# Head softmax attention: scores in two 64-row tiles, all eight half sums added up by TensorE, heads weighed eleven by VectorE and five by GpSimd

## What is computed

```python
q = (x @ Wq.T + bq).reshape(B, S, H, D)
k = (x @ Wk.T + bk).reshape(B, S, H, D)
v = (x @ Wv.T + bv).reshape(B, S, H, D)
scores = jnp.einsum('bqnd,bknd->bnqk', q, k) / jnp.sqrt(jnp.float32(D))
attn = jax.nn.softmax(scores, axis=1)
out = jnp.einsum('bnqk,bknd->bqnd', attn, v)
...
return out @ Wo.T + bo
```

## Time and profile before

| | before |
|---|---|
| median of 3 runs | 2179.37 us (2179.27 to 2180.45) |
| the profiled execution's own time | 2181.45 us |
| its span in the trace | 2178.7 us |
| TensorE busy over the span | 1938.2 us (89%) |
| VectorE | 1730.6 us (79%) |
| GpSimd | 1475.3 us (68%) |
| ScalarE | 1245.5 us (57%) |
| mean granted TensorE clock | 0.949 |

### The profile page before, as it was taken

The page is one execution under the profiler, slowest core; times in us unless marked ns, Lnnn a source line. Parts: engine busy times, 40 slices in busy tenths (PEclk is TensorE's granted clock), DMA queues, the critical chain, the costliest instruction groups (busy, mean ns, idle before and its releaser), DMA issues. The chain is left out here.

```text
span 2178.7 us, 56000 instructions
## 1 busy us (share of the span) xinstructions
PE 1938.2 (89%) x21984; PEld 1282.7 (59%) x21984; DVE 1730.6 (79%) x2433; ACT 1245.5 (57%) x2204; POOL 1475.3 (68%) x1044
## 2 busy tenths in 40 slices
PE   1799937999957999999999999999999996399997
PEld 1566632444424777777777777777777776144443
DVE  5577675666675999999999999999999996666665
ACT  2455424666634666666666666666666664266664
POOL 3100003566564999999999999999999993065564
PEclk9999958999977999999999999999999997699998
DMA  3222205995101000000000000000000000299631
GB/s 121 83 72 71 80 5 113 181 173 131 30 0 40 13 13 13 13 14 11 16 9 16 9 16 9 17 11 15 9 6 9 6 6 1 52 175 185 140 77 39
DMA packets 95317, 108.91 MB, mean 50 GB/s; under 512 B 31600, under 2 KB 56560, under 8 KB 94704
## 3 DMA queue, kind: packets, MB, share of 16 engines
q1 hardware_dynamic: 92256, 103.91, 21.2%
q10 hardware_dynamic: 2832, 1.79, 0.3%
HBM read 88.10 MB, written 17.57 MB: 49 GB/s over the span
## 5 line engine op out<-in xcount | busy, mean ns | idle before, releaser
L1177 POOL TENSOR_TENSOR ffn_exp_sw<-ffn_exp_sg,ffn_exp_wide 128x512 f32<-128x512 f32 x256 | 324.5, 1268 | 573.0 <-DMA ffn_exp_wide<-pair_weights 370.5
L963 DVE TENSOR_REDUCE head_shift<-head_score 128x64 bf16<-128x1024 f32 x512 | 625.2, 1221 | 91.3 <-PE head_score L775 79.1
L925 ACT ACTIVATE head_ex<-head_score 128x1024 f32<-128x1024 f32 x512 | 524.7, 1025 | 188.7 <-PE head_score L797 186.9
L732 POOL TENSOR_TENSOR head_half<-head_ex 128x1024 f32<-128x1024 f32 x256 | 604.2, 2360 | 27.2 <-ACT head_ex L925 27.2
L970 DVE TENSOR_TENSOR head_ex<-head_ex,head_recp 128x1536 f32<-128x1536 f32 x256 | 446.7, 1745 | 4.8 <-ACT head_recp L897 4.8
L807 PE MATMUL head_den<-head_half,c_ident 128*128 128x128 f32 x3072 | 385.3, 275 | 2.9 <-POOL head_half L733 2.7
L807 PEld LDWEIGHTS head_den<-head_half,c_ident 128*128 128x128 f32 x3072 | 363.3, 192 | 6.5 <-POOL head_half L733 3.3
L739 POOL TENSOR_TENSOR head_ex<-head_ex,head_recip 128x512 f32<-128x512 f32 x256 | 328.9, 1285 | 15.3 <-ACT head_recip L899 7.5
L1288 DVE TENSOR_TENSOR ffn_exp_h_parts<-ffn_exp_hidden,ffn_exp_h_parts 128x512 f16<-128x512 f32 x272 | 188.1, 692 | 173.8 <-ACT ffn_exp_h_parts L1248 172.8
L797 PE MATMUL head_score<-head_shift,c_identb 128*128 128x512 bf16 x1024 | 309.9, 384 | 17.6 <-DVE head_shift L963 11.3
L775 PE MATMUL head_score<-att_b_HB,att_b_GR 96*128 96x256 f16 x2048 | 311.0, 274 | 10.4 <-DMA att_b_HB<-b_queries 9.9
(11 more groups left out here) (230 smaller groups left out, 2478.5 us busy)
## 6 DMA issues: line engine op xcount, KB each, us to landing
ffn_exp_wide<-pair_weights SPq DMA_DIRECT2D x256, 256.0 KB, 8.7
a_keys<-band_parts_k SPq DMA_DIRECT2D x14, 295.5 KB, 2.5
att_a_HB<-a_keys SPq DMA_DIRECT2D x56, 73.9 KB
a_queries<-band_parts_q SPq DMA_DIRECT2D x14, 271.5 KB, 3.1
att_a_GR<-a_queries SPq DMA_DIRECT2D x14, 271.5 KB
b_queries<-head_parts_q SPq DMA_DIRECT2D x32, 96.0 KB, 1.6
att_b_HB<-b_queries SPq DMA_DIRECT2D x128, 24.0 KB
b_keys<-head_parts_k SPq DMA_DIRECT2D x24, 96.0 KB, 1.6
```

What stands on the lines that cost most here:

```text
L732: ch.link(pool.tensor_tensor(hf, e[:, 0:8, :], e[:, 8:16, :], ALU.add))
L925: act.activation(ex[:, kt % RING, :, h * QS:(h + 1) * QS], score[:, h, :, :].rearrange("p k (a w) -> p (k a) w", a=NH // 2), ACT.Exp, scal ...
L963: dve.tensor_reduce(shift[:, h, :], score[:, h, :, :].rearrange("p k (a w) -> p w k a", a=NH // 2), AX.XY, ALU.max, negate=True).then_inc( ...
L1177: pool.tensor_tensor(sw[:, g % 2, :], sg[:, g % 2, :], wide[:, g // NU, i, :], ALU.mult).then_inc(sw_ready, 1)
```

## The change

```diff
@@ -42,6 +42,7 @@
 KROWS = GH * D * SLOTS
+RTILE, PROWS = 64, 2 * D * SLOTS
...
-        self.HB = m.sb("HB", [KROWS, 2, NH, P], F16)
-        self.GR = m.sb("GR", [KROWS, 2, NG, S], F16)
+        self.HB = m.sb("HB", [RTILE + PROWS, 2, NH, P], F16)
+        self.GR = m.sb("GR", [RTILE + PROWS, 2, NG, S], F16)
...
-    ON_DVE = 3
-    SLABS = (0, 1, 4, 5, 6, 7)
+    ON_DVE = 11
+    SLABS = range(NH // 2)
     HALVES = S // BLK
-    READS_Q = GH
+    READS_Q, READS_K = GH, 2
...
                     rows = slice(n4 * SLOTS * D, (n4 + 1) * SLOTS * D)
-                    sp.dma_start(HB[rows, n % 2, n4:NH:GH, :], by_row[rows, :, :]).then_inc(q_placed, 16)
+                    at = n4 // 2 * RTILE + n4 % 2 * SLOTS * D
+                    sp.dma_start(HB[at:at + SLOTS * D, n % 2, n4:NH:GH, :], by_row[rows, :, :]).then_inc(q_placed, 16)
                 sp.wait_ge(q_placed, ONE + (n + 1) * (READS_Q * 16))
+
+            def read_k(dram, buf, cols):
+                by_row = dram.rearrange("(g r) s c -> (r s) g c", g=NG)
+                for r in range(2):
+                    sp.dma_start(GR[r * RTILE:r * RTILE + PROWS, buf, :, cols], by_row[r * PROWS:(r + 1) * PROWS, :, :]).then_inc(k_placed, 16)
...
-                sp.dma_start(GR[:, buf, :, kt * P:(kt + 1) * P], k_dram.rearrange("(g r) s c -> (r s) g c", g=NG)).then_inc(k_placed, 16)
-                sp.wait_ge(k_placed, ONE + (n + 1) * 16)
+                read_k(k_dram, buf, slice(kt * P, (kt + 1) * P))
+                sp.wait_ge(k_placed, ONE + (n + 1) * (READS_K * 16))
...
             for i in range(HALVES):
-                sp.dma_start(GR[:, 0, :, i * BLK:(i + 1) * BLK], k_first[i].rearrange("(g r) s c -> (r s) g c", g=NG)).then_inc(k_placed, 16)
+                read_k(k_first[i], 0, slice(i * BLK, (i + 1) * BLK))
...
-                ch.link(pool.tensor_tensor(hf, e[:, 0:8, :], e[:, 8:16, :], ALU.add))
-                pool.tensor_tensor(hf[:, 0:2, :], hf[:, 0:2, :], hf[:, 2:4, :], ALU.add).then_inc(quarter_ready, 1)
+                pool.tensor_tensor(hf, e[:, 0:8, :], e[:, 8:16, :], ALU.add).then_inc(halves_ready, 1)
...
-                e = ex[:, kt % RING, :, :].rearrange("p (g a) q -> p g a q", a=GH)[:, :, ON_DVE, :]
-                pool.tensor_tensor(e, e, recip[:, kt % 2, :][:, None, :].broadcast_to([P, NG, P]),
+                e = ex[:, kt % RING, ON_DVE:NH, :]
+                pool.tensor_tensor(e, e, recip[:, kt % 2, :][:, None, :].broadcast_to([P, NH - ON_DVE, P]),
                                    ALU.mult).then_inc(rest_ready, 1)
...
                 for g in range(NG):
-                    last = pe.matmul(score[:, h, g // 2, (g % 2) * GH * QS:(g % 2 + 1) * GH * QS].rearrange("p (a w) -> p a w", a=GH),
-                                     GR[:, buf, g, kt * P:(kt + 1) * P], HB[:, par, g * GH:(g + 1) * GH, h * QS:(h + 1) * QS],
-                                     start=(g % 2 == 0), stop=False, skip_group_check=True)
+                    for r in range(2):
+                        rows, heads = slice(r * RTILE, r * RTILE + PROWS), slice(g * GH + r * 2, g * GH + r * 2 + 2)
+                        last = pe.matmul(score[:, h, r, :].rearrange("p (e a w) -> p e a w", e=2, w=QS)[:, :, g, :],
+                                         GR[rows, buf, g, kt * P:(kt + 1) * P], HB[rows, par, heads, h * QS:(h + 1) * QS],
+                                         start=(g == 0), stop=False, skip_group_check=True)
                 last.then_inc(score_ready, 1)
...
-                    if i == HH:
+                    if i == ON_DVE:
                         pe.wait_ge(rest_ready, ONE + unit + 2)
...
-                    last = pe.matmul(outp[g * 32:(g + 1) * 32, 0:P], vs[:, buf * BT + kt, at:at + 32], ex[:, kt % RING, n, :],
+                    last = pe.matmul(outp[g * 32:(g + 1) * 32, 0:P], vs[:, buf * BT + kt, at:at + 32], ex[:, kt % RING, i, :],
...
-                e = ex[:, kt % RING, :, :].rearrange("p (g a) q -> p g a q", a=GH)[:, :, 0:ON_DVE, :]
-                dve.tensor_tensor(e, e, recp[:, 0:P][:, None, None, :].broadcast_to([P, NG, ON_DVE, P]), ALU.mult).then_inc(prob_ready, 1)
+                e = ex[:, kt % RING, 0:ON_DVE, :]
+                dve.tensor_tensor(e, e, recp[:, 0:P][:, None, :].broadcast_to([P, ON_DVE, P]), ALU.mult).then_inc(prob_ready, 1)
```

More of the change, by code:

```diff
@@ L661, in head_softmax_attention @@
         ex_ready, den_ready = m.sem("ex_ready", "act"), m.sem("den_ready", "pe", 1)
-        quarter_ready, rest_ready = m.sem("quarter_ready", "pool"), m.sem("rest_ready", "pool", 1)
+        halves_ready, rest_ready = m.sem("halves_ready", "pool"), m.sem("rest_ready", "pool", 1)
         ln_done, recip_ready, prob_ready = m.sem("ln_done", "act"), m.sem("recip_ready", "act", 1), m.sem("prob_ready", "dve", 1)
@@ L666, in head_softmax_attention @@
         out_ready, added = m.sem("out_ready", "pe"), m.sem("added", "dve")
-        pool_chain = m.sem("pool_chain", "pool")
         block = m.ctx.enter_context(nc.Block())
@@ L728, in sum_heads @@
                 e, hf = ex[:, kt % RING, :, :], half[:, kt % 2, :, :]
-                ch = Chain(pool, pool_chain, unit)
                 pool.wait_ge(ex_ready, ONE + 2 * unit + 2)
                 pool.wait_ge(den_ready, ONE + unit)
-                ch.link(pool.tensor_tensor(hf, e[:, 0:8, :], e[:, 8:16, :], ALU.add))
-                pool.tensor_tensor(hf[:, 0:2, :], hf[:, 0:2, :], hf[:, 2:4, :], ALU.add).then_inc(quarter_ready, 1)
+                pool.tensor_tensor(hf, e[:, 0:8, :], e[:, 8:16, :], ALU.add).then_inc(halves_ready, 1)
             def weigh_rest(unit, kt):
                 pool.wait_ge(copy_ready, ONE + unit + 1)
-                e = ex[:, kt % RING, :, :].rearrange("p (g a) q -> p g a q", a=GH)[:, :, ON_DVE, :]
-                pool.tensor_tensor(e, e, recip[:, kt % 2, :][:, None, :].broadcast_to([P, NG, P]),
+                e = ex[:, kt % RING, ON_DVE:NH, :]
+                pool.tensor_tensor(e, e, recip[:, kt % 2, :][:, None, :].broadcast_to([P, NH - ON_DVE, P]),
                                    ALU.mult).then_inc(rest_ready, 1)
@@ L802, in denominator_of @@
             def denominator_of(unit, kt):
-                pe.wait_ge(quarter_ready, ONE + unit + 1)
+                pe.wait_ge(halves_ready, ONE + unit + 1)
                 pe.wait_ge(ln_done, ONE + unit)
@@ L851, in chunk_of @@
                         if is_last(q):
-                            pe.wait_ge(k_placed, ONE + (HALVES + (b + 1) * NQ) * 16)
+                            pe.wait_ge(k_placed, ONE + (HALVES + (b + 1) * NQ) * (READS_K * 16))
                         scores_of(0, 0, 1 - buf if is_last(q) else buf, 1 - par)
@@ L868, in _ @@
                 last.then_inc(v_ready, 1)
-            pe.wait_ge(k_placed, ONE + HALVES * 16)
+            pe.wait_ge(k_placed, ONE + HALVES * (READS_K * 16))
             pe.wait_ge(q_placed, ONE + READS_Q * 16)
```

## The result

The changed kernel takes 2277.11 us (median of 4 runs, 2276.79 to 2278.0) against 2179.91 us before: the ratio is 1.0446, 95% interval 1.0428 to 1.0464. The forecast was 2281, its likeliest case. The profiled execution took 2278.0 us, its span is 2276.2.

What follows compares the result with a forecast made beforehand. Three engines near full before; TensorE alone after. Its 4.31 + 0.45 - 0.41 + 0.37 + 0.12 = 4.84 us a unit (4.79 in the last batch) adds 101.5 us, giving 2281 us; range 2226 to 2312.

Steps and rivals of the forecast that it cites:

- What bounds it before: In the changed stage, GpSimd, the ring through VectorE and TensorE stand within 4%; relieving one gives little.
- TensorE's stall: Before the change, the second maximum waits for VectorE's reduce L963 once per unit: 0.15 us, 0.10 in the last batch.
- rival 1: Boundaries changing rows alone cost nothing; the ring over two units then sets the time: -13 us, 2167 us; chance 0.13.
- Two slabs: In TensorE's denominator, two more slabs are four more matmuls of 0.112 us: +0.45 us a unit.
- The pairs at once: In TensorE's score steps, two row-tile matmuls run at once: 0.235 us a half, saving 0.41 us a unit.
- The boundaries: TensorE's four added passages between full and row tiles, around both score steps, cost 0.092 us each: +0.37 us a unit.
- rival 2: Only going into row tiles, or only going back, costs: 4.64 us a unit, 2231 us; chance 0.10.
- Exposed weight loads: On TensorE, first weight loads after boundaries aren't hidden: +0.10 us for the denominator, +0.02 for 16 bits, per unit.
- The stall gone: The longer denominator ends the wait at the second maximum; GpSimd and VectorE idle 0.6 to 0.9 us a unit.
- The weighings: L970 on VectorE, eleven heads, takes 1.60 us; L739 on GpSimd, five heads, takes 1.56 us.
- The start of the stage: On SyncE, two key-read issues become four ahead of the first queries TensorE waits for: +0.9 us once.
- Rival 3: Row-tile pairs run one after the other and boundaries cost: 5.29 us a unit, 2397 us; chance 0.04.

Runs made afterwards that it cites:

- the run on one tile: The changed kernel with all eight score matmuls of a half on the upper row tile (rows 0 to 47): 2391.93 us.
- the 48-row run: The changed kernel with one extra bf16 matmul of 48 rows and 128 columns in the middle of each denominator: 2369.24 us.
- the run with 96 rows: The changed kernel with the same extra matmul in each denominator, but on 96 rows, which is no row tile: 2306.45 us.

## Why the prediction was right

By its own steps:

- What bounds it before: three engines within 4%. Shown by the runs in so far as relief alone brought little: without the two slabs and the quarter sum 4.39 is reached, 0.07 under 4.458. But the prediction read GpSimd's idle time as mostly the chain's (9.2 us) and passed over the 8.6 us before L739, and it put TensorE's stall down to a ring through VectorE alone. GpSimd held the last batch and half the units before it, as shown above. The forecast doesn't hang on this, since TensorE alone sets the changed kernel's unit; the price of rival 1 does.
- Two slabs: +0.45 forecast; the experiment with two left out gives 0.438.
- The pairs at once, 0.235 a half: a score step of 0.33 less its boundary of 0.09 to 0.10 is 0.23 to 0.24. It was argued from L439 in another stage, and the run on one tile shows it, +0.44 for two halves.
- The boundaries, the term on which all hung: 0.092 assumed for a kind that no row of before had; 0.10 each way in the 48-row run, and 0.53 - 0.44 = 0.09 at the first maximum. Rival 1 needed 0.01 and rival 2 a free side; both fall. The Trainium skill's rule, page "TensorEngine Tiling (Array Packing)", section "Key Properties", that a change of tiling mode drains TensorE, fits these runs for modes that differ in rows alone: each change costs about 0.10 us. That a drain is what takes the time isn't shown.
- Exposed weight loads, 0.12: the denominator takes 1.99, which is 16 x 0.112 = 1.79, and 0.10 for the boundary, and 0.10 for its first load.
- The stall gone, VectorE and GpSimd idle: 0.82 and 0.96 a unit; 0.6 to 0.9 had been forecast, a little too low for GpSimd.
- The weighings 1.60 and 1.56: measured 1.61 and 1.55. The start of the stage +0.9: 0.94 on SyncE's queue, but only 0.2 to 0.5 of it reaches the units.
- The sum 4.84 and 4.79: 4.829 and 4.784. Of the 4 us by which the total was too high, 0.011 x 192 + 0.006 x 64 = 2.5 come from this.

Rival 3 (pairs in turn) gave 2397, and the kernel that forces it measured 2391.93.

## What to carry to other kernels

Matmuls on two 64-row tiles do run at once, but each passage between such a tile and full width costs about 0.10 us (an estimate: as much as 230 columns' streaming, at 0.43 us for two matmuls of 512). So pack rows only where a step saves more than the 0.2 us of its two passages, or where the neighbours use the same tile shape. Before a load is moved from one engine to another in a balanced stage, add up the new sum of each engine with its boundaries and first weight loads: here a relief of 0.5 us on GpSimd was paid with 0.52 on TensorE (from 4.31 to 4.83), which was next. And an order that saves a passage may make a ring of waits that costs more; follow each ring through all engines first.

## What the runs showed of the hardware that was not expected

Two row tiles run side by side even when their matmuls are issued four by four: the half takes 0.34 in place of 0.33, where started in issue order it would take about 0.50 (an estimate: three more distances of 0.056), and on one tile it takes 0.55. The Trainium skill, page "TensorE: Matmul & The Clock Gate", section "Part 3: Packing small matmuls — row/col tiling", says that matmuls start and end in strict program order; for starts on different row tiles this run shows otherwise, and the measurement decides. A float32 weight load behind a 16-bit matmul of 128 columns seems exposed by 0.05 us, with no change of tile shape (argued from the run with 96 rows).
